# A state-space layer between two expert layers: first convolution tap on ScalarE, shared norm statistics, and a block diagonal built by DMA

## What is computed

```
n    = layernorm(x)                       # outer norm, no weights
xn   = layernorm(n) * ln_w + ln_b         # the block's own norm
z, xBC, dt = split(xn @ W_in)             # 512, 544, 64 columns
dt   = softplus(dt + dt_bias)
xBC  = silu(causal_conv4(xBC) + conv_b)   # 4 taps along the tokens
xs, B, C = split(xBC)                     # 512, 16, 16
h_t  = h_{t-1} * exp(-exp(A_log) dt_t) + dt_t * xs_t * B_t
y_t  = h_t . C_t + Dp * xs_t
g    = y * silu(z);  g = g * rsqrt(mean(g*g) + eps) * rms_w
x    = x + n + g @ W_out
```

## Time and profile before

| | us |
|---|---|
| median of 3 runs | 1732.43 (1732.28 to 1732.94) |
| the profiled execution, its own time | 1741.65 |
| its span, first to last instruction | 1739.9 |
| DVE busy | 1325.7 (76%) |
| PE busy | 1276.7 (73%) |
| ACT busy | 724.0 (42%) |
| POOL busy | 654.1 (38%) |

### The profile page before, as it was taken

The page is one execution under the profiler, slowest core; times in us unless marked ns, Lnnn a source line. Parts: engine busy times, 40 slices in busy tenths (PEclk is TensorE's granted clock), DMA queues, the critical chain, the costliest instruction groups (busy, mean ns, idle before and its releaser), DMA issues.

```text
span 1739.9 us, 32954 instructions
## 1 busy us (share of the span) xinstructions
PE 1276.7 (73%) x10560; PEld 961.0 (55%) x10560; DVE 1325.7 (76%) x3687; ACT 724.0 (42%) x1586; POOL 654.1 (38%) x832
## 2 busy tenths in 40 slices
PE   3426999947887787777888777688876551799990
PEld 3416999933545455454545445454544441799990
DVE  5964777758988888888888888898885664577776
ACT  2323555514444444444444444444444220355550
POOL 3873333323434343333424343333422376233330
PEclk9999999968878888888878788888878555899995
DMA  8543333310000000000000000000000022333328
GB/s 216 183 168 88 95 97 94 84 34 13 16 22 13 25 14 18 20 16 21 15 24 14 24 13 18 20 16 22 16 16 11 33 86 89 89 94 93 94 81 302
DMA packets 86838, 104.66 MB, mean 60 GB/s; under 512 B 18192, under 2 KB 66320, under 8 KB 86672
## 3 DMA queue, kind: packets, MB, share of 16 engines
q1 hardware_dynamic: 67856, 59.31, 13.2%
q0 software_dynamic: 14208, 39.05, 6.1%
q10 hardware_dynamic: 4608, 4.20, 0.7%
HBM read 50.88 MB, written 43.23 MB: 54 GB/s over the span
## 4 chain that ended last, share of the span: by engine, by line
PE 35%; DVE 22%; SPq 13%; POOL 9%; DMA 8%; issue 8%; ACT 5%; another core or an unknown queue 0%; POOLq 0%; DVEq 0%; ACTq 0%
SPq L1068 11%; PE bank L641 11%; PE bank L655 11%; DMA yg<-ychosen 5%; POOL disp L545 4%; ACT y L1115 4%; PE bank L1175 4%; DVE cv L876 3%; DVE cv L879 3%; PE bank L1242 2%; POOL arena L1028 2%; PE bank L1225 2%; DVE X L816 2%; PE bank L624 2%; DMA y<-y 1%
## 5 line engine op out<-in xcount | busy, mean ns | idle before, releaser
L590 POOL DMA_INDIRECT ychosen<-arena,didx x144 | 139.8, 971 | 295.1 <-ACT arena L687 280.1
L641 PE MATMUL bank<-arena,weights 128*128 128x128 f16 x3456 | 221.0, 221 | 0.0
L655 PE MATMUL bank<-weights,arena 128*128 x1728 | 211.5, 273 | 0.0
L641 PEld LDWEIGHTS bank<-arena,weights 128*128 x3456 | 203.3, 99 | 0.6 <-issue 0.3
L676 ACT ACTIVATE arena<-bank 128x512 f32<-128x512 f32 x144 | 86.0, 597 | 240.9 <-issue 140.3
L717 DVE TENSOR_TENSOR arena<-arena 128x512 f32<-128x512 f32 x144 | 99.8, 693 | 105.8 <-ACT arena L676 104.4
L1206 PE MATMUL bank<-arena,cst 128*128 128x512 f32 x256 | 172.4, 810 | 0.0
L655 PEld LDWEIGHTS bank<-weights,arena 128*128 128x128 f16 x1728 | 163.2, 98 | 16.4
L545 POOL DMA_INDIRECT disp<-arena,sloti x128 | 132.6, 1036 | 65.2 <-issue 39.8
L876 DVE TENSOR_SCALAR cv<-U,vec 128x128 f32<-128x128 f32 x160 | 141.7, 948 | 0.0
L1014 POOL TENSOR_TENSOR Hs<-Hs,dd 64x512 f32<-64x512 f32 x32 | 34.3, 1071 | 282.4 <-DVE yi L916 268.3
(11 more groups left out here) (168 smaller groups left out, 2646.7 us busy)
## 6 DMA issues: line engine op xcount, KB each, us to landing
arena<-disp SPq DMA_DIRECT2D x144, 129.5 KB
arena<-in_w SPq DMA_DIRECT2D x16, 512.0 KB
yg<-ychosen SPq DMA_DIRECT2D x32, 256.0 KB, 2.8
y<-y SPq DMA_DIRECT2D x512, 16.0 KB, 1.8
arena<-ychosen SPq DMA_DIRECT2D x32, 256.0 KB, 5.9
X<-in_x SPq DMA_DIRECT2D x32, 128.0 KB, 4.6
out<-X ACTq DMA_DIRECT2D x32, 128.0 KB, 6.1
ychosen<-arena,didx POOLq DMA_INDIRECT x144
```

The lines of the kernel that those rows point to most:

```text
L590: pool.indirect_dma_start(ychosen, bass.IndirectOffsetOnAxis(ap=didx[:, t % NIDX:t % NIDX + 1], axis=0), ysb[t % YB][:, :], None).then_inc ...
L641: mm = pe.matmul(o, chunk(where, 2 * ("hl".index(w) * WN + c * HID + m * P), P), v, start=c == 0 and n_ == 0, stop=c == KD - 1 and n_ == 2)
L655: mm = pe.matmul(o, x, chunk(where, 2 * ((2 + "hl".index(w)) * WN + c * D), D), start=c == 0 and n_ == 0, stop=c == KH - 1 and n_ == 2)
```

## The change

- `conv`: the tap of the current token and the bias are computed by ACT straight from PSUM, at the end of `channels`: five instructions, into `cv`, which now has two buffers. DVE adds the other three taps (15 instructions; the 5 of L876 are gone).
- Norms: one set of statistics. POOL raises `var + eps` and `var (1 + eps) + eps^2` to -1/2 together, since the second norm of a normed row has the same mean and a scale that follows from the same variance. DVE forms `xn` directly from `X`; the residual `X + xm` is one ACT instruction on `X` with a scale and a bias for each row. The steps `norm2`, `xm` and `mb` are gone, and so is POOL's second power.
- `dt_out`: log1p as a polynomial of degree 9 in e; 11 chained DVE instructions in place of 15.
- `cbs`: the product with `bm` is issued once for each sequence and accumulated in PSUM; the DVE sum L898 is gone.
- `bd`: POOL clears it once. Its blocks are filled by four DMAs a tile of 32x512 from SP (`spread`), in place of ACT's four instructions. Its layout is now by sequence, then head; `intra` reads it in that order.

```diff
+LOG1P = (0.99999997, -0.49999493, 0.33319097, -0.24842983, 0.19106008, -0.13663247, 0.07822596, -0.02950524, 0.00523269)
...
-        cv = sb("cv", [P, (NB + 1) * P])
+        cv = [sb(f"cv{p}", [P, (NB + 1) * P]) for p in range(2)]
...
-        NTAP = DC * (NB + 1)
+        NTAP = (DC - 1) * (NB + 1)
...
             def combine(k, p):
 
                 ca.at(k)
+                after(dve, "m_xm", k)
                 dve.wait_ge(S(f"yg_{p}"), k * 8 + (16 - 8 * p))
                 for j in range(2):
                     ca.link(dve.scalar_tensor_tensor(out=Xk(k), in0=yg[p][:, j * D:(j + 1) * D], scalar=wts[:, ds(k * 2 + j, 1)],
...
                 ca.link(dve.bn_stats(ma[:, 0:6], Xk(k)))
                 hold(dve, "dve")
                 ca.link(dve.bn_aggr(ma[:, 6:8], ma[:, 0:6]))
-                dve.tensor_scalar(ma[:, 8:9], ma[:, 7:8], EPS, None, ALU.add).then_inc(S("m_va"), 1)
+                dve.tensor_scalar(ma[:, 8:9], ma[:, 7:8], EPS, None, ALU.add)
+                dve.tensor_scalar(ma[:, 9:10], ma[:, 7:8], 1.0 + EPS, EPS * EPS, ALU.mult, ALU.add).then_inc(S("m_va"), 1)
 
             def norm(k, p):
 
                 dve.wait_ge(S("m_ra"), k + 1)
-                ca.link(dve.tensor_scalar(xm[:, :], Xk(k), ma[:, 6:7], ma[:, 9:10], ALU.subtract, ALU.mult))
-                ca.link(dve.bn_stats(mb[:, 0:6], xm[:, :]))
-                hold(dve, "dve")
-                ca.link(dve.bn_aggr(mb[:, 6:8], mb[:, 0:6]))
-                dve.tensor_scalar(mb[:, 8:9], mb[:, 7:8], EPS, None, ALU.add).then_inc(S("m_vb"), 1)
-
-            def norm2(k, p):
-                ca.link(dve.tensor_tensor(Xk(k), Xk(k), xm[:, :], ALU.add))
+                dve.tensor_scalar(xn[:, :], Xk(k), ma[:, 6:7], ma[:, 11:12], ALU.subtract, ALU.mult).then_inc(S("m_xn"), 1)
+                dve.tensor_scalar(ma[:, 12:13], ma[:, 10:11], 1.0, None, ALU.add)
+                ca.link(dve.scalar_tensor_tensor(out=ma[:, 13:14], in0=ma[:, 6:7], scalar=-1.0, in1=ma[:, 10:11],
+                                                 op0=ALU.mult, op1=ALU.mult))
+                dve.sem_inc(S("m_shift"), 1)
                 ca.done()
-                dve.wait_ge(S("m_rb"), k + 1)
-                dve.tensor_scalar(xn[:, :], xm[:, :], mb[:, 6:7], mb[:, 9:10], ALU.subtract, ALU.mult)\
-                    .then_inc(S("m_xn"), 1)
 
...
                 dve.wait_ge(S("m_e"), k + 1)
-                cb_.link(dve.tensor_scalar(den_, e_, 2.0, None, ALU.add))
-                cb_.link(dve.reciprocal(den_, den_))
-                cb_.link(dve.tensor_tensor(s_, e_, den_, ALU.mult))
-                cb_.link(dve.tensor_tensor(s2, s_, s_, ALU.mult))
-                cb_.link(dve.tensor_scalar(q, s2, 1.0 / 15, None, ALU.mult))
-                for c in (13, 11, 9, 7, 5, 3):
-                    cb_.link(dve.scalar_tensor_tensor(out=q, in0=q, scalar=1.0 / c, in1=s2, op0=ALU.add, op1=ALU.mult))
-                cb_.link(dve.scalar_tensor_tensor(out=l, in0=q, scalar=1.0, in1=s_, op0=ALU.add, op1=ALU.mult))
-                cb_.link(dve.tensor_scalar(v, v, 0.0, None, ALU.max))
-                cb_.link(dve.scalar_tensor_tensor(out=dt_[p][:, :], in0=l, scalar=2.0, in1=v, op0=ALU.mult, op1=ALU.add))
+                cb_.link(dve.tensor_scalar(q, e_, LOG1P[-1], None, ALU.mult))
+                for c in LOG1P[-2::-1]:
+                    cb_.link(dve.scalar_tensor_tensor(out=q, in0=q, scalar=c, in1=e_, op0=ALU.add, op1=ALU.mult))
+                cb_.link(dve.scalar_tensor_tensor(out=dt_[p][:, :], in0=v, scalar=0.0, in1=q, op0=ALU.max, op1=ALU.add))
...
                 dve.wait_ge(S("m_hist"), k + 1)
-                for c in range(DC):
+                dve.wait_ge(S("m_cv"), k + 1)
+                for c in range(DC - 1):
                     for j in range(NB + 1):
-                        o = cv[:, j * P:(j + 1) * P].rearrange("p (b t) -> p b t", t=QT)
-                        u = taps(p, c, QT)[:, j]
-                        if c == 0:
-                            m = dve.tensor_scalar(o, u, vc(V_CW, j * DC, 1), vc(V_CB, j, 1), ALU.mult, ALU.add)
-                        else:
+                        o = cv[p][:, j * P:(j + 1) * P].rearrange("p (b t) -> p b t", t=QT)
+                        if c:
                             dve.wait_ge(S("m_tap"), k * NTAP + ((c - 1) * (NB + 1) + j + 1))
-                            m = dve.scalar_tensor_tensor(out=o, in0=u, scalar=vc(V_CW, j * DC + c, 1), in1=o,
-                                                         op0=ALU.mult, op1=ALU.add)
-                        m.then_inc(S("m_tap"), 1)
+                        dve.scalar_tensor_tensor(out=o, in0=taps(p, c, QT)[:, j], scalar=vc(V_CW, j * DC + c, 1), in1=o,
+                                                 op0=ALU.mult, op1=ALU.add).then_inc(S("m_tap"), 1)
...
                 dve.wait_ge(S("m_cbp"), k + 1)
                 dve.tensor_copy(bt[p][:, :], banks[2][:, 0:B * DS_])
-                ce.link(dve.tensor_reduce(cbr[:, :], banks[2][:, P:2 * P].rearrange("p (b t) -> p t b", b=B), AX.X, ALU.add))
-                dve.tensor_tensor(cb[p][:, :], cbr[:, :], const(C_QM), ALU.mult).then_inc(S("m_cb"), 1)
+                dve.tensor_tensor(cb[p][:, :], banks[2][:, P:P + QT], const(C_QM), ALU.mult).then_inc(S("m_cb"), 1)
...
             def finish(k, p):
                 dve.wait_ge(S("m_o"), k + 1)
                 dve.wait_ge(S("m_rr"), k + 1)
+                dve.wait_ge(S("m_xm"), k + 1)
...
             all_stored(pool, 0)
             pool.memset(taps(1, QT, DC - 1), 0.0).then_inc(S("m_hist_set"), 1)
-            def power(sem_in, sem_out, ap_in, ap_out, k):
+            pool.memset(bd[:, :], 0.0).then_inc(S("m_bd_set"), 1)
...
...
                 if "C" in parts:
                     state(i, p)
                 if "A" in parts:
-                    power("m_va", "m_ra", ma[:, 8:9], ma[:, 9:10], i + 2)
+                    power("m_va", "m_ra", ma[:, 8:10], ma[:, 10:12], mhalf[:, 0:2], i + 2)
                 if "D" in parts:
                     add_moved(i - 1, 1 - p)
-                if "A" in parts:
-                    power("m_vb", "m_rb", mb[:, 8:9], mb[:, 9:10], i + 2)
...
+            def spread(k, p):
+
+                sp.wait_ge(S("m_dtx"), k + 1)
+                after(sp, "m_intra", k * 2)
+                for b in range(B):
+                    sp.dma_start(bd[b * QT:(b + 1) * QT, b * DI:(b + 1) * DI], dtx[p][b * QT:(b + 1) * QT, :])\
+                        .then_inc(S("m_bd"), 16)
+
             all_stored(sp, 0)
             load(0, 0)
             load(1, 1)
-            load(2, 0)
-            move(0)
-            load(3, 1)
-            move(1)
-            for k in range(2, NT):
+            sp.wait_ge(S("m_bd_set"), 1)
+            spread(0, 0)
+            for k in range(NT):
                 if k + 2 < NT:
                     load(k + 2, k % 2)
                 move(k)
+                if k + 1 < NT:
+                    spread(k + 1, (k + 1) % 2)
...
             def normed(k, p):
 
+                act.wait_ge(S("m_shift"), k + 1)
+                act.activation(Xk(k), Xk(k), ACT.Identity, scale=ma[:, 12:13], bias=ma[:, 13:14]).then_inc(S("m_xm"), 1)
...
             def channels(k, p):
                 act.wait_ge(S("m_up"), k + 1)
                 act.activation(taps(p, DC - 1, QT)[:, 0:NB], banks[1][:, :].rearrange("p (j b t) -> p j b t", b=B, t=QT),
-                               ACT.Copy).then_inc(S("m_U1"), 1)
+                               ACT.Copy)
                 act.activation(taps(p, DC - 1, QT)[:, NB], banks[2][:, 0:P].rearrange("p (b t) -> p b t", t=QT),
-                               ACT.Copy).then_inc(S("m_U"), 1)
+                               ACT.Copy)
+                after(act, "m_g", 2 * (k - 1))
+                for j in range(NB + 1):
+                    u = banks[1][:, j * P:(j + 1) * P] if j < NB else banks[2][:, 0:P]
+                    m = act.activation(cv[p][:, j * P:(j + 1) * P], u, ACT.Identity, scale=vc(V_CW, j * DC + DC - 1, 1),
+                                       bias=vc(V_CB, j, 1))
+                    if j == NB - 1:
+                        m.then_inc(S("m_U1"), 1)
+                m.then_inc(S("m_U"), 1)
+                act.sem_inc(S("m_cv"), 1)
...
                     for g in range(4):
                         act.wait_ge(S("m_Lp"), i * 4 + (g + 1))
                         act.activation(R[p][:, g * GRP:(g + 1) * GRP], banks[4 + g % 2][:, :], ACT.Exp).then_inc(S("m_L"), 1)
-                        if g == 1:
-
-                            act.wait_ge(S("m_dtx"), i + 1)
-                            after(act, "m_intra", i * 2)
-                            for b in range(B):
-                                m = act.activation(bd.rearrange("p (h b e) -> p h b e", b=B, e=HP)[:, :, b, :],
-                                                   by_head(dtx[p][:, :]), ACT.Copy, scale=const(C_BM)[:, b:b + 1])
-                            m.then_inc(S("m_bd"), 1)
...
                 if g == 0:
```

(7 more changed lines are left out.)

26 lines of the change are left out of this document (11 added, 15 removed).

## The result

| | before | after |
|---|---|---|
| median, runs of one chip, us | 1732.36 (1731.96 to 1732.94) | 1787.97 (1777.42 to 1797.30) |
| profiled execution, us | 1741.65 | 1786.69 |
| its span, us | 1739.9 | 1784.9 |

The change makes the kernel slower: the ratio is 1.0319, with a 95% interval of 1.0261 to 1.0377. The direction was forecast; the size was not: 1828 was predicted, and the rise is 56 us instead of 96.

A forecast was written before the change was run, and what follows sets the result against it. A chain of waits closing once a turn, 30.14 us a lap, bounds the kernel. Legs of 6.2, 16.9, 7.5 and 3.1 make 33.7: +100 over 28 laps, +1 first turns, -5 last, net +96, so 1828 us, range 1772 to 1866.

The forecast's parts named there:

- The lap as the account: Mamba part's chain of waits, closing once a turn: 30.14 us before, 33.7 forecast, over 28 laps +100 us.
- leg C: SP's DMA issues up to the load: four more at 0.62 us each, 4.99 us rising to 7.5.
- leg D: Load to combine: sharing the DMA engines with the copy's data adds 0.2 us, to 3.1.
- leg A: Combine to G: one tiny DVE instruction and a second column in POOL's power add 0.3 us, to 6.2.
- B2: ACT, from its copy of the channels to the tanh: 0.65 us plus 1.8 for five taps, 2.45 forecast.
- split product: PE, four small products replacing one for the batch sum: under 0.5 us more, in front of a wait.
- Leg B1: PE's matmuls from G's transposes to ACT's copy: slowed by longer idling for G, 11.94 us forecast.
- the last turns: Last two turns of the Mamba part: no load on the lap and L1132 on the chain, -5 us.
- Rival 1: Mamba lap doesn't lengthen and DVE's relief shows: laps of 29.3 us, near 1705; chance 0.08.
- Rival 2: PE stays quick while SP's issues cost full price: laps of 31 to 32 us, near 1765; chance 0.06.
- Rival 3: PE reads `bd` slower in short runs: 2 us more a lap, 35.7, near 1885; chance 0.06.
- the signs listed: Expected in the profile: DVE idle 4 us or more before combine, PE over 4 for G, L1101 about 12 behind L1234.

The follow-up runs named there:

- load-first run: Changed kernel with SP issuing the next tile's load behind the move but ahead of the four diagonal DMAs: 1705.74 us, ratio 0.9814.
- the filler: Changed kernel with 18 extra, unused 128x128 transposes on PE ahead of its wait for silu: 1833.49 us, ratio 1.0499.
- the kernel with the early load: Changed kernel with SP issuing the load ahead of the move of an earlier tile and of the diagonal's DMAs: 1690.13 us, ratio 0.9741.
- the extra matmuls: Unused PE matmuls ahead of a wait; 18 ahead of silu's wait gave 1833.49 us in the changed kernel, 1655.23 with the load ahead of the move.

## Why the prediction was right, and where it was too high

**The lap as the account.** It held: the 28 laps give +52.4 us, what lies around them -7.4, together the 45.0 between the two spans. The loss is where the prediction put it, in leg C on SP, and DVE's relief vanished under PE's path, as said.

**Leg C.** Forecast 7.5, measured 7.64. The load-first run shows it causally: with the same DMAs behind the load it is 5.10. Against this stood the rule of the Trainium skill, page "DMA: Bandwidth & Descriptors", section "Rules for kernel authors", to issue early and wait late, by which the copy would be free. Here the trace disagrees with what I made of that rule: the copy's data cost next to nothing (leg D 2.99 for 2.88), its four issues, 0.63 us apart in the chain above, cost all of leg C's growth.

**Legs A and D.** 6.23 for 6.2 and 2.99 for 3.1. The power takes 0.94 on the chain where the one before took 0.80, so it gives 0.14 of leg A's 0.22. That the second column is the reason is not shown: in the changed kernel POOL's other power, of one column, takes 0.93 in the mean.

**The tap.** ACT's five take 1.86, forecast 1.8 from L1095. B2 came to 2.37 for 2.45. DVE's 15 take 7.31 and end before ACT's taps begin (928.58 and 928.82 in the lap shown), so ACT is the later one: in none of the 28 laps does it idle before the tanh. That the DVE instruction with two SBUF inputs is slowed beside POOL, and the Trainium skill, page "SBUF — State Buffer", section "Who interferes with whom", agree. Over the 28 laps the same 420 instructions are busy for 204.3 us where they took 112.5 (the rows below, before and after), so that 92 of the 127.6 us that L876 took come back. They stayed off the path.

```profile
L876 DVE TENSOR_SCALAR cv<-U,vec 128x128 f32<-128x128 f32 x140 | 127.6, 974 | 0.0
L879 DVE SCALAR_TENSOR_TENSOR cv<-U,vec,cv 128x128 f32<-128x128 f32 x420 | 112.5, 340 | 0.0
```

```profile
L865 DVE SCALAR_TENSOR_TENSOR cv<-U,vec,cv 128x128 f32<-128x128 f32 x420 | 204.3, 557 | 0.0
```

**log1p and batch sum.** `dtx` ends at 906.75 (906.07 and 0.68 us) and SP reaches the first of the four issues at 907.23, so the wait cost nothing, as said. The split product was put at under 0.5 us more on PE. It is mis-sized: L1266 takes 46.3 us over the 28 laps, 1.65 a turn, where L1272 took 17.3, 0.62 a turn. It lies on PE's path to G, in front of a wait, so this too cost nothing, but it fed the next point.

**Leg B1 failed.** The step was: "PE's work in it does not [grow], so the idle is 4 to 6 us and I take the slowest of the three turns, 11.94." Two things were wrong in it. PE's work did grow, from 10.8 to 13.0 us busy: 1.0 by the split product, while the clock behind silu fell from 0.77 to 0.69. The stretch itself grew by 1.8 us, from 14.3 to 16.1, and not by over 2. And ahead of that stretch the wait for silu had changed, 3.63 us in every turn. Each kernel with the tap on ACT and that wait not filled has 3.62 to 3.66 there, each with it on DVE a mixture of 1.7 to 4.5: ACT's copy, its taps and the tanh now always follow PE's projection. I had looked at the wait for G alone.

That idle time ahead of the stretch lowers the clock in it is what the filler shows; that the even length does it is not shown. In the kernel before, waits of 2.13 and 2.18 us are followed by 0.64 and 0.98, and the norms, log1p and batch sum alone, with 2.5 us there in the mean, also bring the clock to 0.73 and B1 to 10.1. PE so came later to G, idled 1.7 to 4.5 us, no more than before, and was at full speed behind G in 11 of the 28 turns, where it had been in 6. The filler ahead of silu's wait shows by experiment that the two stretches trade: with that stretch quick, B1 is 11.59 and the lap 33.41, close to the 33.7 forecast.

The step's own assumption also held in the run with the diagonal by DMA alone, where B1 is 11.40. So the 46 us are not a leg's own work saved: the slow stretch had moved to where, with PE waiting for a late G anyway, it cost nothing.

**The rest of the sum.** In the span: laps -48 against the forecast, the last turns +3 (-2.1 for -5), first turns and the part's start 0, the second expert layer -6.5; 96 comes down to 45. The median rose 11 more than the profiled executions did, since that of before lay 9 above its median and that of after 1 below.

**Rivals.** Rival 1 (faster, near 1705) failed for the reason given, the price of an issue. Once the load is moved, 1705.74 is what comes. Rival 2, PE stays quick, 31 to 32 us, near 1765, was half right: 32.01 lies on its upper end, and PE was quick in 11 turns of 28. I gave it 0.06, since I saw no reason for PE to be quick with a later G; the reason was the slow stretch ahead of G. Rival 3 failed: over the 28 laps L1225 before and L1218 after take the same 116.4 us for 1792 matmuls, so PE reads the new layout at no cost. Of the signs listed, DVE's idle ahead of the combine (3.1 us in the mean, 4 or more in one lap), the idle for G (over 4 in 6 of 26 turns, not nearly all) and the 12 us of L1101 (two turns) did not come.

## What to carry to other kernels

An issue has a price on the queue that issues it, 0.62 to 0.63 us each here. Before a copy moves from an idle engine to a DMA queue, look what stands behind it there, and put first what a chain waits for. Here the place of one load among four small DMAs was worth 5%.

Where DVE, SP and PE are all close to the lap's length, relief on one shows little while the next stands beside it: 4.56 us a turn taken off DVE's place on the chain brought 0.3%. What the tap or the norms alone would bring in the kernel with the early load, or with the extra matmuls, was not run.

The same matmuls behind G took 9.24 us at a granted clock of 1.00 and 10.93 at 0.84, and the waits of PE decided which. So ask of every wait of PE in the loop, not only of the one on the path, what its length becomes, and where the slow stretch that follows will lie.
